# One more VectorE operation between each pair of recurrences and its product with C, in a selective scan with attention behind it

## The reference

```python
x_dbl = jnp.einsum('kcd,bkdl->bkcl', x_proj_w, xs)        # xs: rows, columns, both reversed
dts, Bv, Cv = jnp.split(x_dbl, [R, R + N], axis=2)
dt = jax.nn.softplus(jnp.einsum('kdr,bkrl->bkdl', dt_proj_w, dts) + dt_proj_b[None, :, :, None])
def step(h, inp):                                          # one position
    dA = jnp.exp(dt_t[..., None] * A)
    h = dA * h + dt_t[..., None] * B_t[:, :, None, :] * u_t[..., None]
    y = jnp.einsum('bkdn,bkn->bkd', h, C_t)
# y of the four directions and Ds * xs are summed, normalised, gated and projected; x is added
```

## Time and profile before

| | us |
|---|---|
| median of three runs | 9437.26 |
| lowest, highest | 9434.93, 9440.56 |
| profiled execution, its own time | 9426.04 |
| its span | 9424.2 |
| TensorE busy | 8659.1 |
| VectorE busy | 7371.5 |
| ScalarE busy | 6096.1 |
| GpSimd busy | 3293.4 |

### The profile page before, as it was taken

One profiled execution on the slowest core, in us unless ns is written; L12 is line 12 of the kernel. 1 busy time (PEld: TensorE's weight loads), 2 busy tenths in 40 slices (PEclk: granted clock), 3 DMA queues, 4 the chain that ended last, 5 costly groups with the idle time before them and its releaser, 6 DMA issues. The chain is left out here.

```text
span 9424.2 us, 104196 instructions
## 1 busy us (share of the span) xinstructions
PE 8659.1 (92%) x26436; PEld 4640.1 (49%) x26436; DVE 7371.5 (78%) x8225; ACT 6096.1 (65%) x7436; POOL 3293.4 (35%) x1874
## 2 busy tenths in 40 slices
PE   7899988999889998899988999889998899988999
PEld 3336733367333673336733367333673336633366
DVE  6987769876698766987679876798767987679876
ACT  6765667656675566755667556675566755677555
POOL 2860028600385003850038500385003850038500
PEclk9999999999999999999999999999999999999999
DMA  1320013200132001320013200132001320023200
GB/s 52 116 79 11 11 53 111 80 11 11 55 115 76 11 10 55 116 75 10 12 58 111 75 10 12 60 114 71 10 12 60 116 68 10 12 66 110 68 12 12
DMA packets 286693, 503.21 MB, mean 53 GB/s; under 512 B 142155, under 2 KB 143215, under 8 KB 253431
## 3 DMA queue, kind: packets, MB, share of 16 engines
q1 hardware_dynamic: 286199, 497.81, 17.7%
HBM read 467.99 MB, written 29.47 MB: 53 GB/s over the span
## 5 line engine op out<-in xcount | busy, mean ns | idle before, releaser
L1363 DVE TENSOR_TENSOR pl<-pf,ph 128x1024 fp32r<-128x1024 f32 x1024 | 1254.1, 1225 | 1014.2 <-ACT ph L1003 1008.0
L1217 DVE TENSOR_TENSOR_SCAN h<-ps,h,dbu 128x512 f32<-128x512 f32 x1536 | 1882.7, 1266 | 52.2 <-POOL dbu L1068 29.9
L1068 POOL TENSOR_TENSOR dbu<-bs,du 128x1024 f32<-128x1024 f32 x768 | 1808.5, 2370 | 54.1 <-POOL du L1059 54.1
L1003 ACT ACTIVATE ph<-pf 128x1024 fp32r<-128x1024 f32 x1024 | 1085.7, 1060 | 753.5 <-PE ps L695 753.2
L867 ACT ACTIVATE ps<-dt,negA 128x512 f32<-128x512 f32 x1536 | 1037.9, 687 | 720.4 <-DVE h L1217 720.1
L1023 POOL MEMSET sqb<- 64x512 f32 x16 | 8.3, 519 | 3985.4 <-issue 3980.4
L997 ACT ACTIVATE pf<-ps 128x1024 f32<-128x1024 f32 x1024 | 1051.0, 1026 | 534.9 <-PE ps L682 534.9
L1347 DVE TENSOR_REDUCE mx<-ps 128x1 f32<-128x512 f32 x1792 | 1167.9, 683 | 78.7 <-PE ps L600 60.5
L1225 DVE TENSOR_TENSOR hc<-h,ps 128x1024 f32<-128x1024 f32 x768 | 937.5, 1221 | 113.9 <-PE ps L481 20.0
L481 PE MATMUL ps<-xhl,selr 128*128 128x512 f32 x1536 | 756.2, 577 | 259.8 <-DVE hc L1225 259.5
L1053 POOL TENSOR_TENSOR dt<-dt,ze 128x1024 f32<-128x1024 f32 x256 | 604.5, 2361 | 1044.0 <-ACT dt L860 1043.9
(11 more groups left out here) (200 smaller groups left out, 14514.2 us busy)
## 6 DMA issues: line engine op xcount, KB each, us to landing
bs<-rows SPq DMA_DIRECT2D x256, 1024.0 KB, 5.2
bs<-rows SPq DMA_DIRECT2D x512, 256.0 KB, 6.1
xa<-in_x SPq DMA_DIRECT2D x130, 256.0 KB, 2.9
xb<-in_x SPq DMA_DIRECT2D x130, 128.0 KB, 3.0
out<-fa SPq DMA_DIRECT2D x64, 256.0 KB, 2.1
rdb<-rden SPq DMA_DIRECT2D x56, 192.0 KB, 3.6
out<-fa SPq DMA_DIRECT2D x64, 128.0 KB, 2.4
xhl<-ct SPq DMA_DIRECT2D x256, 8.0 KB
```

The source lines that it names most:

```text
L1003: A(ph[:, mp % 2, :, :], pf[:, mp % 2, :, :], ACT.Copy).then_inc(S["ph_ready"], 1)
L1068: pool.tensor_tensor(dbu[:, q, :, :], bs[par][:, q, :, :], du[:, r:r + 1, :].to_broadcast([P, 2, T]), ALU.mult).then_inc(S["dbu_ready"], 1)
L1217: dve.tensor_tensor_scan(h[:, j, ::step], ps[:, 2 + e, ::step], dbu[:, q, e, ::step], h[:, j, end:end + 1], ALU.mult, ALU.add)\
L1363: TT(pl[:, mp % 2, :, :], pf[:, mp % 2, :, :], ph[:, mp % 2, :, :].bitcast(F32), ALU.subtract)\
```

## The change

On VectorE the body of the scan is written out: the softplus of g + 1 stands between pair 0's recurrences and their product with C; pair 2's first recurrence stands between pair 1's recurrences and their product; the residue of g + 2 stands between pair 2's second recurrence and its product. The low half comes last.

On ScalarE 1 + exp comes straight after exp, ahead of the store of xs and the high copy. In the second half the copy of the rest (`add_y1`) moves behind 1 + exp.

On TensorE the dt products of g + 2 come ahead of pair 1's spread in both halves. In the second half the fold of the rest for chunk g moves out of body g into body g + 1 (or behind the last body), behind pair 1's spread.

```diff
@@ TensorE @@
-                def old_rest_col(c, g):
+                def rest_col(k, c, g):
                     pe.wait_ge(S["y1_added"], g + 1)
-                    mm(ps[:, 0, :], eye1[R:P, :], ycol[R:P, c * T:(c + 1) * T], start=True, stop=False)
-                def rest_col(k, g):
-                    if k == 1:
-                        pe.wait_ge(S["y1_added"], g + 1)
+                    if k == 3:
+                        mm(ps[:, 0, :], eye1[R:P, :], ycol[R:P, c * T:(c + 1) * T], start=True, stop=False)
...
-                        spread(1, *now, at, g)
                         if after:
                             dtproj(*after, at + 2, g + 2)
+                        spread(1, *now, at, g)
+                        if at > EV:
+                            rest_col(*before, g - 1)
                         old_col(now[1], None if at == EV else g)
                         spread(2, *now, at, g)
                         add_col(g)
-                        if now[0] == 3:
-                            old_rest_col(now[1], g)
                         if nxt:
                             spread(0, *nxt, at + 1, g + 1)
                         sum_second(g)
-                        rest_col(now[0], g)
                         return
...
-                    spread(1, *now, at, g)
                     if after:
                         dtproj(*after, at + 2, g + 2)
+                    spread(1, *now, at, g)
                     sum_first(*now, g)
@@ ScalarE @@
                     if before:
-                        if at > EV:
-                            add_y0(*before, g - 1)
-                        add_y1(*before, g - 1)
+                        (add_y0 if at > EV else add_y1)(*before, g - 1)
...
                         soft_relu(g + 2)
                         soft_exp(g + 2)
+                        soft_one(g + 2)
+                    if at > EV:
+                        add_y1(*before, g - 1)
+                    if after:
                         if at + 2 in STORE:
                             store_xs(after[1])
                         if at + 2 < EV:
                             copy_high(at + 2, g + 2)
-                        soft_one(g + 2)
                         soft_log(par, g + 2)
@@ VectorE @@
-                    for q in range(NP):
-                        s = g * NP + q
-                        scans(now[0], q, s)
-                        times_c(q, s)
-                        if q == 0 and nxt:
-                            if not before:
-                                residue(g + 1)
-                            softplus(1 - par, g + 1)
+                    k, s = now[0], g * NP
+                    scans(k, 0, s)
+                    if nxt:
+                        if not before:
+                            residue(g + 1)
+                        softplus(1 - par, g + 1)
+                    times_c(0, s)
+                    scans(k, 1, s + 1)
+                    scans(k, 2, s + 2, (0,))
+                    times_c(1, s + 1)
+                    scans(k, 2, s + 2, (1,))
                     if after:
-                        if at + 2 < EV:
-                            low_half(at + 2)
                         residue(g + 2)
+                    times_c(2, s + 2)
+                    if after and at + 2 < EV:
+                        low_half(at + 2)
```

More of the change, by code:

```diff
@@ L585, in _ @@
                 run_chunks(pe, b, body)
+                rest_col(K - 1, 0, g_0 + G - 1)
                 barrier(pe, b, 0)
@@ L1207, in softplus, with scans @@
                     STT(dt[par][:, :, :], ps[:, 6:8, :], -1.0, dt[par][:, :, :], ALU.mult, ALU.add).then_inc(S["dt_ready"], 1)
-                def scans(k, q, s):
+                def scans(k, q, s, halves=(0, 1)):
                     step = -1 if k >= 2 else 1
@@ L1212, in scans @@
                     dve.wait_ge(S["dbu_ready"], s + 5)
-                    for e in range(2):
+                    for e in halves:
                         j = 2 * q + e
```

## The result

The changed kernel takes 9520.4 us (9515.1 to 9524.3, four runs) against 9437.2: a ratio of 1.0088, 95% interval 1.0070 to 1.0105. It is slower by 83 us, where 9434 was forecast with 9398 to 9468 as the range.

The account below looks back on a forecast made before the run. Prediction took the scan as bound by VectorE, losing 0.60 us a body in gaps; a 0.64 us wait on ScalarE's chain replaces them. Terms summed to -0.35 us an image, -3 us over 8: 9434 us, range 9398 to 9468.

Parts of the forecast that it names:

- What goes: VectorE in the scan: the 0.20 us gap between each recurrence pair and its product is filled, saving 0.60 us a body.
- a rival: VectorE: gaps aren't filled, independent operations start no sooner behind a recurrence than the product does; 9477 us, chance 0.06.
- What comes in its place: VectorE waits 0.64 us per body before the residue for ScalarE's 1 + exp; second-half body 13.44 us against 13.40.
- Low half: VectorE, first half: standing directly ahead of the recurrence, it adds 0.84 us, making bodies 14.28 us.
- Direction 3: TensorE level with VectorE at product 2: 0.0 to 0.2 us on each of 6 bodies, 0.10 taken.
- 1 + exp moved up: ScalarE: left behind the storing and high copy, 1 + exp would make the residue wait 1.46 us more in store bodies.
- TensorE: Second half: |x| could start at 5.66, ScalarE reaches it at 6.57, so covered by 0.9 us; direction 3 costs 0.10 a body.
- the chain starts late through TensorE's dt products: First half: later x products delay dt products and |x|; 0.3 to 0.4 us late gives 9465 to 9476, chance 0.14.
- Edges: Per image: body 0 costs 0.4 us, the cleared state column before directions 1 and 3 0.1 twice, last two bodies 0.
- sign of the uncertainty: Chances for the whole kernel: faster 0.24, same within 0.2% 0.54, slower 0.22.

Follow-up runs that it names:

- The run of the first half alone with the idle stretch broken: Kernel before with the change in directions 0 and 2 only, TensorE's sum of the second products held until 1 + exp is made: 9431.5 us, ratio 1.0001.
- the run on the last fold: Changed kernel, with the rest's fold of the last body but one made at its own end again: 9513.4 us, ratio 1.0078 against the kernel before.
- the first split run: Changed kernel, but in directions 0 and 2 TensorE holds its sum of the second products until 1 + exp is made: 9514.2 us, 1.0078 against the kernel before.

## Why the prediction was wrong

**Right.** *What goes:* 0.60 us of gaps per body; the operations behind a recurrence started 1.18 after it. The Trainium skill's rule that the next VectorE operation can't start before the pipeline is empty (VectorE: DVE Perf Modes, "The DRAIN you can't avoid") was weighed as a rival. The same section says that an operation that isn't held starts earlier, which the prediction left out, and that is what the trace shows: with a product 1.21 us long the next recurrence starts 1.13 after it, and the gaps could be filled.
*What comes in its place:* forecast 0.64 us of waiting in front of the residue, measured 0.58 in the second half and 0.68 in the first. The second half's body was forecast at 13.44, measured 13.41. The run of the first half alone with the idle stretch broken (1.0001) shows the balance without falls.
*Low half:* forecast 14.28, measured 14.35. The low half's own extra is 14.35 - 13.49 = 0.86 (13.49 is body 16, with the same 0.68 wait), 0.84 forecast. By the Trainium skill's rule on held operations (same page, "Two Vector instructions with no wait between them") two of the three late starts of before stay, and the trace agrees: the low half starts 1.24 after the product, the recurrence 0.73 after the low half, and the softplus 2.37 after that. The other 0.07 is |x|, which starts 0.72 behind the decay there, 0.62 taken.
*Direction 3:* 0.12 a body, 0.10 forecast. Product 2 starts 1.25 after the residue there, behind pair 2's spread, and 1.14 in direction 1.
*1 + exp moved up:* without it 1.29 us more in a store body, forecast 1.46 less the overlap won behind exp.

**Wrong.** The step that failed is *TensorE*, and with it the rival "the chain starts late through TensorE's dt products", which got 0.14. Its place and sign were right: "ScalarE arrives at 6.57", |x| at 6.5 to 6.6, a tie without slack. What was missing is why the tie would be lost. All of TensorE's durations were taken from rows at full clock, and that the clock would stay up was never asked, though the change moves TensorE's idle time. With the dt products ahead of pair 1's spread and the softplus early, TensorE no longer waits in front of the dt products and the sum; it waits 1.8 us in one piece for product 2, which stands behind the residue's wait, where it had waited 0.7. In the bodies with a fall the x products and the start of the sum then run at half clock. The dt products run at full clock but start 1.7 us late (6.1 against 4.4 after the body's start), |x| starts at 8.0 where 6.57 was forecast (6.65 in a body without a fall), and a body without slack pays 1.38 (0.83 more at the residue, 0.45 at a decay, and 0.1). That is 5.1 us in bodies 1 to 13 of the first image, 5.5 where four bodies are hit, and some 0.6 in body 14, which the sum had at 0.
*Edges* were mis-sized: body 0 cost 1.0, not 0.4, and the last bodies 3.0 against 0. There too the sum was made at full clock. TensorE's fold at 3.68 us instead of 1.98 is 1.7 of the 3.0; in the run on the last fold, the one image without a fall in these bodies took 29.6 us for them, 0.2 more than before the change.

The sign of the uncertainty was wrong as well: a fall only cost time in every run here, and the range, 36 us below the forecast and 34 above, treated the risk as even.

**Open.** What decides in which body the clock falls. In the changed kernel it falls about every third body with the same idle time in each; broken up there, it falls in every second body of direction 1, with the idle times that the changed kernel has there without falls. The kernel before shows the same: in body 13 of each of its eight images TensorE stood idle for 2.5 us in front of L529, and the clock fell there in five images and not in three. So the length of the idle time doesn't decide it alone. The falls are evenly spaced, too: 44.4 us from start to start in the first image, which is the length of three bodies there, one of them slow, and 27.3 us in direction 1 of the first split run, two bodies. So when a stretch comes counts beside how long it is, and a fall that is avoided or moved shifts what comes behind it; that is a reading of these rows, and no run tests it. The runs show that idle time of TensorE has to do with it (1.0057 to 1.0001 by one hold), not the rule by which. Also open are how the 83 us split between the halves, since each alone costs 0.6 to 0.7% and both together 0.9%, and what lengthens the stages outside the scan.

## What to carry to other kernels

Filling a dependent gap on the busiest engine is worth its size only if the loop through the other engines isn't as long already: close the loop (here recurrence, decay chain, residue) before counting the gaps, and fill those that lie outside it. When a change shifts work past an engine's waits, write down that engine's idle stretches before and after; here a TensorE stretch that grew from 0.7 to 1.8 us, with the sum nearly the same, went with a halved clock behind it in every third body, and what was due right then set the price, 0.1 to 2.7 us a fall. Look at all repetitions of a stage, since one of them can miss what the others show.

## What the runs showed of the hardware

TensorE's granted clock fell to 1.2 GHz for 3.4 us at a time in a stage in which it was 87% busy (167.99 of 192 us), after idle times of 1.8 us, and in other orders after 0.87 and 0.67 us in one body (first split run, direction 1). The same stretches were also passed without a fall. More matmuls (0.47 us more in each of 16 bodies) made the kernel no slower: 9510 against 9520 us. And a fall that was avoided in one stage came in a later one that was the same instruction for instruction.
